# Attention in pairs of heads on half the array, results scattered by the experts, and rebuilt gates and bridge in a macaron block

## The reference, cut to what matters

```python
x = x + 0.5 * ffn(layernorm(x))
x = x + attn(layernorm(x))
x = x + 0.5 * ffn(layernorm(x))
# ffn, for each token n and its two experts e with weights combine[n, e]
g, u = split(x[n] @ gate_up[e].T)
out[n] += combine[n, e] * ((silu(g) * u) @ down[e].T)
# attn, for each head
scores = where(causal, q @ k.T / 4, -inf)
y = softmax(scores) @ v
```

## Time and profile before

| what | value |
|---|---|
| three runs | 1754.65, 1756.78, 1756.82 us, median 1756.78 |
| span of the profiled execution | 1753.7 us, 28131 instructions |
| PE, PEld, DVE, ACT, POOL busy | 76, 54, 60, 48, 29% of the span |
| DMA moved | 87.98 MB, 50 GB/s over the span |

### The profile page before, as it was taken

One profiled execution on the slowest core, in us unless ns is written; L12 is line 12 of the kernel. 1 busy time (PEld: TensorE's weight loads), 2 busy tenths in 40 slices (PEclk: granted clock), 3 DMA queues, 4 the chain that ended last, 5 costly groups with the idle time before them and its releaser, 6 DMA issues. The chain is left out here.

```text
span 1753.7 us, 28131 instructions
## 1 busy us (share of the span) xinstructions
PE 1325.4 (76%) x8236; PEld 952.2 (54%) x8237; DVE 1049.7 (60%) x3069; ACT 838.7 (48%) x1616; POOL 515.6 (29%) x783
## 2 busy tenths in 40 slices
PE   6327999931486999999999999999989029999600
PEld 6316787731375555555555555555578017888500
DVE  4783444323786777777777777777564873444344
ACT  2313444400243677777777777777732314444300
POOL 0454434257454000000000001110020644444266
PEclk9999999955698899999999999999995559999855
DMA  5312332253000000000000000000002402233244
GB/s 168 132 36 70 90 95 90 81 158 96 24 1 0 1 1 0 0 0 0 0 0 0 0 0 0 0 0 0 1 1 96 145 6 88 91 94 94 73 124 150
DMA packets 66328, 87.98 MB, mean 50 GB/s; under 512 B 11248, under 2 KB 53488, under 8 KB 66288
## 3 DMA queue, kind: packets, MB, share of 16 engines
q1 hardware_dynamic: 53232, 51.83, 9.2%
q0 software_dynamic: 13056, 35.67, 7.0%
HBM read 56.01 MB, written 31.46 MB: 50 GB/s over the span
## 5 line engine op out<-in xcount | busy, mean ns | idle before, releaser
L1280 ACT ACTIVATE a_prob<-a_psS 128x1024 f32<-128x1024 f32 (+3 forms) x384 | 308.1, 812 | 135.0 <-PE a_psS L1275 97.8
L1228 DVE CUSTOM_DVE_ANT_0 a_psM<-a_psM,a_causal 128x128 f32<-128x128 f32 (+3 forms) x512 | 250.6, 496 | 99.3 <-PE a_psM L1221 94.7
L1221 PE MATMUL a_psM<-a_KT,a_shared 128*128 128x512 f32 (+3 forms) x576 | 234.0, 411 | 8.0 <-ACT a_KT L1204 7.5
L1231 DVE TENSOR_REDUCE a_mpart<-a_psM 128x1 f32<-128x512 f32 x256 | 176.6, 691 | 94.1 <-PE a_psM L1221 90.0
L650 PE MATMUL m_psG<-m_wgu,m_x_hi 128*128 x576 | 197.1, 424 | 14.5 <-issue 12.6
L1175 POOL CAST a_stack<-a_QK 128x256 fp32r (+1 forms) x64 | 27.9, 464 | 604.0 <-PE a_psR L1251 600.4
L1272 PE MATMUL a_psS<-a_shared,a_KT 128*128 128x512 f32 (+3 forms) x576 | 193.7, 382 | 0.0
L1298 PE MATMUL a_psO<-a_prob,a_VP 128*32 128x512 f32 (+3 forms) x1536 | 175.4, 498 | 1.2 <-ACT a_OT L1317 1.2
L1221 PEld LDWEIGHTS a_psM<-a_KT,a_shared 128*128 128x128 f32 x576 | 110.7, 194 | 91.2 <-DVE a_mpart L1228 74.0
L612 POOL DMA_INDIRECT m_xg<-xn,m_idx x144 | 140.1, 973 | 65.9 <-POOL m_idx L609 57.8
L668 DVE TENSOR_TENSOR m_h<-m_act_g,m_psG 128x256 f32<-128x256 f32 x144 | 60.6, 421 | 164.3 <-ACT m_act_g L665 164.3
(11 more groups left out here) (207 smaller groups left out, 2693.3 us busy)
## 6 DMA issues: line engine op xcount, KB each, us to landing
ys<-m_y SPq DMA_DIRECT2D x144, 128.0 KB, 1.8
xn<-m_XN SPq DMA_DIRECT2D x8, 1024.0 KB, 4.4
m_w_stage<-gate_up SPq DMA_DIRECT2D x16, 512.0 KB, 3.4
X<-x SPq DMA_DIRECT2D x4, 1024.0 KB, 7.3
m_w_stage<-down SPq DMA_DIRECT2D x16, 256.0 KB, 3.6
out<-X SPq DMA_DIRECT2D x8, 512.0 KB
m_xg<-xn,m_idx POOLq DMA_INDIRECT x144
m_yg<-ys,m_cidx POOLq DMA_INDIRECT x128
```

The costliest lines, as they stand in the source:

```text
L1221: do("pe", "mx_done", lambda: e.matmul(psM[b][:, 0:n], QT[r][:, qt * P:(qt + 1) * P], KT[r][h][:, first:first + n], start=True, stop=True))
L1228: do("dve", "max_done", lambda: e.tensor_tensor_reduce(psM[b][:, 0:n], psM[b][:, 0:n], causal[:, HALF - n:HALF], 1.0, -3e38, ALU.add, ALU. ...
L1231: do("dve", "max_done", lambda: e.tensor_reduce(out, psM[b][:, 0:n], AX.X, ALU.max))
L1280: do("act", "exp_done", lambda: e.activation(prob[s % 4][:, :, 0:n], psS[b][:, :, 0:n], ACT.Exp))
```

## The change

It keeps the reference's computation and rewrites nearly every stage.

- **Heads in pairs on row halves.** Head 0 of a pair lies on array rows 0 to 48, head 1 on rows 64 to 112, 48 or 49 rows each (high, low and high part of 16 channels, and one row for the maximum). A head's scores go to a PSUM bank of its own. The work of a pair is nine steps: `FILLS` (query-major scores, one two-bank tile `psM` a step, read by one or two DVE reductions), `STEPS` (key-major, one bank a head and step, three banks) and `VALUES`. `FILLS` run 15 steps ahead (`LEAD`). Values are split into two column halves a head (`z`), four equal column groups. The causal mask is four small bf16 matmuls in five of nine fills, and POOL's `affine_select` on the exponentials in place of L1275. Stacks, their transposes and the transposes of the output are gone: `project` writes q and k channel-major to DRAM (`QD`, `KD`), SP loads them stacked, results go to DRAM (`OD`), and POOL scales them in batches of four pairs.
- **Experts.** 71 blocks, three in flight (`AHEAD`, `BEHIND` = 3), without a loop. POOL gathers by `slot_u` itself and also scatters each block's rows (L889) to the token's own place in `ys`; the copy of `psY` is DVE's. The block's expert number is loaded before `output` of an earlier block. In the first mixture the split weights are also written to DRAM, and the second reads them back.
- **Combine.** SP reads four tiles' results with two plain DMAs (`Rows.fetch`). The first combine is inside `project` ("bridge"), which makes packs of 512 tokens: six packs of q and k (two of them with neighbouring channels exchanged, so that the rotation is two products and a sum) and v with the second gate's part.
- **Gates.** Logits come from a transposed copy of `x` given by the host (first) or out of the projections (second); routing works in two halves with counts carried by PE, bf16 one-hots and fewer operations.
- One scaling of means by -1 is a `scalar_tensor_tensor` with a tile of ones.

```diff
-    do("pool", "idx_ready", lambda: e.tensor_copy(idx[j][:, :], slot_u[:, bass.ds(i, 1)]))
-    if on("pool"):
-        wait("idx_ready")
-    do("pool", f"gathered{j}", lambda: e.indirect_dma_start(
-        xg[j][:, :], None, xn_d[:, :], bass.IndirectOffsetOnAxis(ap=idx[j][:, 0:1], axis=0)), 16)
...
+def gather(b):
+    if b >= R:
+        pool.wait_ge(x_turned, b - R + 1)
+    pool.indirect_dma_start(xg[b % R][:, :], None, xn_d[:, :],
+                            bass.IndirectOffsetOnAxis(ap=slot_u[:, b, 0:1], axis=0)
+                            ).then_inc(gathered[b % R], 16)
+def scatter(b):
+    pool.wait_ge(y_copied, b + 1)
+    pool.indirect_dma_start(ys_d[:, :], bass.IndirectOffsetOnAxis(ap=slot_u[:, b, 1:2], axis=0),
+                            y[b % R][:, :], None).then_inc(stored[b % R], 16)
...
+for b in range(NB + BEHIND):
+    if b < NB:
+        gate_and_up(b)
+    for n in turns(b):
+        turn_x(n)
+    if b + 1 < NB:
+        expert[b + 1] = pe.value_load(block_expert[0:1, b + 1:b + 2], min_val=0, max_val=E - 1)
+    if b >= BEHIND:
+        output(b - BEHIND)
+    if 1 <= b <= NB:
+        turn_h(b - 1)
...
-wait_apart(pool, cidx_ready, n * R + j + 1, passed)
-for k in range(2):
-    pool.indirect_dma_start(yg[k][j][:, :], None, ys_d[:, :],
-                            bass.IndirectOffsetOnAxis(ap=cidx[j][:, k:k + 1], axis=0)
-                            ).then_inc(got[j], 16)
...
+def fetch(self, sp, g):
+    for k in range(2):
+        sp.dma_start(self.tiles[k][g % self.n][:, :, :], self.source[k, :, self.W * g:self.W * g + self.W, :]
+                     ).then_inc(self.landed[g % self.n], 16)
...
-do("pe", "mx_done", lambda: e.matmul(psM[b][:, 0:n], QT[r][:, qt * P:(qt + 1) * P],
-                                     KT[r][h][:, first:first + n], start=True, stop=True))
...
-for h in range(2):
-    m = e.matmul(psS[b][:, h, 0:n], KT[r][h][:, kt * P:(kt + 1) * P],
-                 QT[r][:, qh * HALF + first:(qh + 1) * HALF], start=True, stop=not diagonal)
-    if diagonal:
-        m = e.matmul(psS[b][:, h, 0:P], mask[0][:, :], mask[1][:, :], start=False, stop=True)
...
+LEAD = 15
+ACROSS = 5
+FILLS = (((0, 0, 128), (2, 0, 384)), ((1, 0, 256), (5, 512, 256)), ((3, 0, 512),), ((4, 0, 512),), ((5, 0, 512),),
+         ((6, 0, 512),), ((7, 0, 512),), ((4, 512, 128), (6, 512, 384)), ((7, 512, 512),))
+STEPS = (((0, 0),), ((0, 1), (0, 3)), ((0, 2), (1, 6)), ((1, 0),), ((1, 1),), ((1, 2),), ((1, 3),), ((1, 4),),
+         ((1, 5), (1, 7)))
+VALUES = (((0, 0),), ((1, 0), (1, 1)), ((2, 0),), ((3, 0), (2, 1)), ((4, 0),), ((5, 0),), ((6, 0),), ((7, 0),),
+          ((8, 0), (8, 1)))
+PER = 9
+TOGETHER = ((0, 1), (2, 3), (4, 5), (6, 7), (8,))
...
+QT = [sb(f"QT{r}", [P, T], F32R) for r in range(NK)]
+psM = [ctx.enter_context(nc.psum_tensor(f"h_psM{j}", [P, 2, HALF], F32)) for j in range(NM)]
+psS = [ctx.enter_context(nc.psum_tensor(f"h_psS{j}", [P, HALF], F32)) for j in range(NS)]
+psO = ctx.enter_context(nc.psum_tensor("h_psO", [P, 2, HALF // 2], F32))
...
+for qt, first, n in order.FILLS[i]:
+    diagonal = first + n == (qt + 1) * P
+    for h in range(2):
+        rows = slice(Q * h, Q * h + K3)
+        m = pe.matmul(out[:, h, at:at + n], pairs.query(p)[rows, qt * P:(qt + 1) * P], pairs.key(p)[rows, first:first + n],
+                      start=at == 0, stop=not diagonal)
+    at += n
+    if diagonal:
+        blocks.append(at // P - 1)
+if blocks:
+    m = masked_scores(out, blocks)
...
+if n == 0 and x >= NS:
+    pe.wait_ge(s_read, x - NS + 1)
+rows = slice(Q * h, Q * h + K3 + 1)
+m = pe.matmul(psS[x % NS][:, at:at + width], pairs.key(p)[rows, kt * P:(kt + 1) * P],
+              pairs.query(p)[rows, qh * HALF + first:(qh + 1) * HALF], start=True, stop=True)
+if n == len(order.STEPS[i]) - 1:
+    m.then_inc(s_filled, 1)
...
+def across(p, out):
+    pe.wait_ge(least_done, p + 1)
+    return pe.matmul(out[0:16, 0:P], least[p % 2][:, :, :].rearrange("p h t -> p (h t)"), ident[:, :],
+                     start=True, stop=True)
...
+for step, n in order.VALUES[i]:
+    qh, kt = order.STEPS[step][n]
+    first, width = order.span(qh, kt)
+    at = order.place(step, n)
+    for h in range(2):
+        for z in range(2):
+            j = 2 * h + z
+            src = prob[(k - i + step) % NP][:, h, at:at + width]
+            m = pe.matmul(psO[32 * j:32 * j + DH + 1, qh, first // 2:HALF // 2],
+                          VP[p // PR][:, kt, 2 * (p % PR) + h, :],
+                          src.rearrange("p (t z c) -> p t z c", z=2, c=Q)[:, :, z, :],
+                          start=kt == 0, stop=(i == 2 or (i, n) == (PER - 1, 1)))
...
+for steps in order.TOGETHER:
+    ks = [PER * p + i for i in steps]
+    new = [k + LAG for k in ks if k + LAG < order.n]
+    for k in new[0:1]:
+        scores(k)
+    for k in ks:
+        values(k)
+    for k in new[1:]:
+        scores(k)
+    for k in new:
+        ahead(k)
...
+for k in range(order.n):
+    p, i = k // PER, k % PER
+    for h in range(2):
+        x = at_s[k] + h
+        act.wait_ge(s_filled, x + 1)
+        act.activation(prob[k % NP][:, h, :], psS[x % NS][:, :], ACT.Exp).then_inc(s_read, 1)
+    if i == order.ACROSS and p + 1 < G:
+        x = at_row[p + 1]
+        act.wait_ge(s_filled, x + 1)
+        row_of(psS[x % NS], p + 1).then_inc(s_read, 1)
+    if i == LAG - 1 and p >= 1:
+        out(p - 1)
...
+for qt, first, n in order.FILLS[i]:
+    out = least[r][:, :, qt] if qt < 4 else part[r][:, first // HALF, :, qt - 4]
+    m = dve.tensor_reduce(out, psM[k % NM][:, :, at:at + n], AX.X, ALU.max, negate=True)
+    at += n
+m.then_inc(m_read, 1)
...
+for at in order.diagonal(i):
+    block = prob[k % NP][:, :, at:at + P]
+    m = pool.affine_select(block, block, [[0, 2], [1, P]], ALU.is_ge, 0.0, 0, -1)
+m.then_inc(masked, 1)
...
+for g in range(NG):
+    pe.wait_ge(xlo_done, 2 * g + 2)
+    for n in range(3):
+        pack(g, n)
+    if g + 1 < NG:
+        turn(g + 1)
+    for n in range(3, NP):
+        pack(g, n)
+        if g == 0 and n == 3:
+            pe.wait_ge(flo_done, 10)
+        value(g, n - 3)
+    value(g, 3)
...
+for a in (2 * u, 2 * u + 1):
+    for c in range(CC):
+        m = pe.matmul(psW[:, a, 0:CE], rows(g)[:, c, a * P:(a + 1) * P], w_c[:, c, :], start=c == 0,
+                      stop=c == CC - 1)
+m.then_inc(summed, 1)
...
+def low_places(self, dve, q, half=None):
...
+    for t in range(a, b):
+        for k in range(2):
+            m = dve.tensor_scalar(self.low(2 * t + k), self.consts["iota_fb"][:, :], self.lo[:, t, k:k + 1],
+                                  float(sh.Y0 // P + t + sh.NT * k), ALU.is_equal, ALU.mult)
...
+pool.wait_ge(whi_done, 3 * e + n + 1)
+pool.tensor_tensor(l, l.bitcast(F32), h.bitcast(F32), ALU.subtract).then_inc(wlo_done, 1)
...
+dve.scalar_tensor_tensor(lx[:, PER * g:PER * g + PER, E:M], mv[j][:, :, 0].unsqueeze(2).to_broadcast([P, PER, M - E]),
+                         -1.0, consts["ones"][:, 0:PER * (M - E)].rearrange("p (t m) -> p t m", m=M - E),
+                         ALU.mult, ALU.mult)
```

More of the change, by code:

```diff
@@ L204, in moe @@
+def moe(nc, sh, name, gate, X, weight, out_d, xn_d, ys_d, wgu, wdn, consts, out_done, early, w_d, results):
+    NT, E, C, F, CC, NB = sh.NT, sh.E, sh.C, sh.F, sh.CC, sh.BLOCKS
     ctx = ExitStack()
@@ L742, in moe @@
-            out_t = out_d.rearrange("(t p) c -> p t c", p=P) if out_d is not None else None
-            if extra:
-                extra.open(c1)
-            block = c1.enter_context(nc.Block(f"{name}_combine"))
+            R, W, yg, got = results.n, results.W, results.tiles, results.landed
+            NG = NT // W
+            half = [sb1(f"half{j}", [P, C]) for j in range(2)]
+            half_done, o_done = sem1("half_done"), sem1("o_done")
+            out_t = out_d.rearrange("(t p) c -> p t c", p=P)
@@ new lines, in three, with __init__, place @@
+def three(e, out, hi, lo, wts):
+    k = 0
+    n = 3 * len(hi)
+    for a, b in ((hi, wts[0]), (lo, wts[0]), (hi, wts[1])):
+        for c in range(len(hi)):
+            m = e.matmul(out, a[c], b[c], start=(k == 0), stop=(k == n - 1))
+            k += 1
+    return m
+class Area:
+    def __init__(self, nc, ctx, name, words):
+        self.nc, self.words = nc, words
+        self.whole = ctx.enter_context(nc.sbuf_tensor(name, [P, words], F32))
+        self.base = nc.sbuf_base - 4 * words
+    def place(self, name, shape, at, d=F32):
+        return self.nc.alloc_sbuf_tensor_at(name, [P] + shape, d, offset=self.base + 4 * at)
@@ L1533, in program @@
[L1533 to L1538 removed]
+        out_done, wg_in, *o_out = (ctx.enter_context(nc.semaphore(n)) for n in ("out_done", "wg_in", "o_out0", "o_out1"))
+        lent = Area(nc, ctx, "spare", SPARE)
+        spare = lent.whole
+        early = Early(nc, sh, ctx, spare, (wq_down, wk_down, wv_down), ups, wc, rope, KD, consts["ones"])
+        X = sb("X", [P, sh.NT, sh.C])
+        weight, middle = sb("weight", [P, 2, sh.NT]), sb("middle", [P, sh.CC, sh.M])
```

(14 more changed lines are left out.)

2646 lines of the change are left out of this document (1497 added, 1149 removed).

## The result

The changed kernel takes 1230.97 us (median of four runs, 1227.33 to 1236.37) beside 1756.28 of the kernel before; the ratio is 0.7013, with a 95% interval of 0.6995 to 0.7031. The profiled execution has a span of 1230.0 us. The forecast was 1189 in a range of 1110 to 1300.

What follows compares the result with a forecast made beforehand. PE was taken to bound heads and experts, DVE's chain the gates, POOL's indirect DMAs the combines. Stage terms 103 + 195 + 130 + 445 + 68 + 195 + 50 = 1186, with 3 outside 1189 us; range 1110 to 1300.

Steps and rivals of the forecast that it cites:

- its own case: Whole kernel: 1120 to 1250 us, from 13.0 to 15 us a pair and 2.5 to 2.92 a block; chance 0.67.
- Heads, 445 forecast: Heads stage: PE 12.8, DVE 11.6, ACT 11.6 us a pair; 13.5 a pair with coupling, 445 us for 708.
- The 0.7 added for coupling: Heads: 0.7 us a pair added because PE, DVE and ACT lie within 1.2 us and are coupled.
- Row halves one behind the other: Heads, rival: the two heads' scores run in turn, 106 us more, 1295 us; chance 0.16.
- Better overlap: Rival: masks and mode changes free, heads 54 us less; experts at POOL's 2.50, 34 less; 1101 us; chance 0.06.
- Experts, 2 x 195 forecast: Both experts stages: PE keeps the bound at 2.74 us a block, 71 blocks, 195 us each for 210 and 208.
- the forecast's low end of 2.50: Experts: POOL's two indirect DMAs a block at 1.25 us each, if a scatter costs what a gather costs.
- the high end of 2.92: Experts: a block costs what it does in the kernel before, 2.92 us.
- DVE held up by POOL: First gate and projection, rival: POOL's work delays DVE, +20 and +40 us, 1249 us; chance 0.09.
- Combine with projection, 130 and 130: First combine and projection: PE 104 us for eight packs, about 26 us ahead of it, 130 us for 212.
- Slower than before, by the clock: TensorE, rival: the clock grant falls in the heads and PE's terms double; all of them give 2095 us; chance 0.02.
- 0.99 and 1.00 where it is always busy: TensorE's clock: granted 0.99 and 1.00 in stages where PE is always busy, 0.50 and 0.61 where it is not.

Runs made afterwards that it cites:

- e9: Changed kernel with two TensorE semaphore increments a block instead of four in both experts stages; 1145.9 us, ratio 0.6600; run again, 1236.7 us, ratio 0.7053.
- e10: Changed kernel without the four mask products of each diagonal step in the heads; 1146.3 us, ratio 0.6580.
- e8: Changed kernel with score and mask products of both heads of a pair reading rows 0 to 63; 1632.0 and 1702.8 us.
- e11: Changed kernel with two increments a block instead of four and without the heads' mask products; 1144.6 us, ratio 0.6577.
- e2: Changed kernel with SyncE's plain store in place of GpSimd's scatter in the second experts stage; 1191.5 us.
- e5: Changed kernel with a plain store and a second gather of each block in place of the scatter, second experts stage; 1218.9 us.
- e6: Changed kernel with SyncE's plain load in place of the gather, scatter kept, second experts stage; 1187.2 us.

## Why the prediction was right, point by point

The total is 42 us over the forecast, inside its own case of 1120 to 1250. In part that is luck: the experts are 65.5 us over, outside the +26 that this case allowed them, by a mechanism that no rival had, and the other stages give 22 back. Without the hold-up e9 and e10 take 1146 us, 43 under the forecast.

- **Heads, 445 forecast, 428 measured: right, by terms that offset.** I added up PE's starts from 520 to 820 us, 23.8 pairs, each instruction up to the start of the next, waits included: query-major scores 3.1 us a pair and key-major 4.3 (2.6 and 2.6 forecast), masks 0.43 (1.3 with their changes of type), values 4.7 (5.7), together 12.6 for PE's 12.8. The scores were taken 2.2 us too low: a step of two heads, taken at 0.235 us, costs 0.24 at best, but 0.34 behind values. Masks and values were too dear by nearly as much; eight value matmuls of 256 columns take 0.44 us for 0.55. The 0.7 added for coupling did not come, so a pair takes 12.6 for 13.5, 29 us over 32 pairs; slow pairs at the lower clock (the first takes 15.4) are some of what the forecast had nothing for. The Trainium skill (TensorEngine Tiling (Array Packing), Key Properties) has tiles of different rows run in parallel; by that rule, the trace agrees, with starts 3 ns apart and 0.24 us for two.
- **Row halves one behind the other (rival, 1295): did not come**, and its price was right: 3.3 us a pair forecast, and 3.5 in e8 where it has the full clock.
- **Better overlap (rival, 1101): in part.** Masks cost little, but a pair takes 12.3 to 13.1, not 11.8. The experts' part, POOL's pace, came in e9 to e11 alone.
- **DVE and ACT in the heads**: groups by form, `L1920` answers to the earlier trace rows. A reduction over two banks takes 1216 ns, 1.04 ns a column and 0.15 an instruction, as forecast; an exponential takes 600 for 595.

```profile
L1895 ACT ACTIVATE spare<-h_psS 128x512 f32<-128x512 f32 x576 | 306.4, 600 | 89.3 <-PE h_psS L1802 87.7
L1920 DVE TENSOR_REDUCE h_part<-h_psM 128x2 f32<-128x1024 f32 x160 | 191.5, 1216 | 12.1 <-PE h_psM L1781 11.9
```

- **Experts, 2 x 195 forecast, 232 and 223 measured: the step that failed.** "PE keeps the bound: 71 x 2.74" is wrong twice. (Its terms add up to 2.77, which is 4 us over both stages.) PE needs 2.53, less than POOL's pair of DMAs, a gather at 0.97, a scatter at 0.99 and 0.30 after each, 2.57: without the hold-up POOL sets the pace, 182 us (e10), the forecast's low end of 2.50. With it a block takes 3.13, above the high end of 2.92. The forecast had counted POOL's DMAs as time of POOL alone; e2, e5 and e6 show that two of them a block can also delay what other engines learn of PE. Its first stage also has 7.7 us between the last output product and the projection, for which the term had nothing.
- **DVE held up by POOL (rival, 1249): true in kind, small in extent.** Of the 64 one-hots of the first gate 55 take 0.25 us and nine take 1.3, those that run beside POOL's last nine splits of 1.27. Timelines of POOL and DVE at that place:

```profile
60.81 2.49 POOL L740 TENSOR_TENSOR wgu<-wgu,wgu 128x512 fp32r<-128x512 f32 x2
59.59 5.00 DVE L216 TENSOR_SCALAR spare<-iota_fb,m_lo 128x128 bf16<-128x128 bf16 x4
```

They cost 9 us, in the gate, whose term held nevertheless. The Trainium skill (SBUF — State Buffer, Terms, on the shared port pair) has each of the two hold the other up for a whole instruction: by that rule, the trace agrees. In the second gate, with no POOL work beside them, all 64 take 0.25.
- **Combine with projection, 130 and 130; last combine, 50 and 44; gates 103 and 68 for 98.7 and 73.8: right.** The last stage moves 294 GB/s, near the upper of the two rates the term was bounded by. In the second gate the raise is PE's: 128 matmuls of 266 columns take 36 us from the first start to the last, for 33.
- **Slower than before, by the clock (rival, 0.02): did not come**, but its price was real: e8, with nearly all of the heads at 0.50, takes 897 us there, although PE is always busy. "0.99 and 1.00 where it is always busy" was thus no safe sign, and left out that the first gate had 1.00 with PE busy 54 of 145 us. The changed kernel's heads start at 0.50 and have 1.00 from 500 on, but for dips (0.91 in 540 to 560, 0.87 in 850 to 889).
